# Second attention in turns of grouped heads, with transposed values, minima and masked scores on VectorE, and expert rows gathered in two groups

## What is computed

```python
    x = x + gb * _L0_ffn_ref(h, ...)
    ...
    h = _layernorm(x, axis=-1) * (1 + ca) + sa
    x = x + ga * _L1_attn_ref(h, ...)
    ...
    for qs in range(0, S, WINDOW):
        ...
        k_c = jnp.concatenate([k[:, :, :meta_end], k[:, :, ls:qe]], axis=2)
        ...
        scores = jnp.einsum('bhqd,bhkd->bhqk', q_c, k_c) * scale
        scores = jnp.where(allowed[None, None], scores, -jnp.inf)
        attn = jax.nn.softmax(scores, axis=-1)
        chunks.append(jnp.einsum('bhqk,bhkd->bhqd', attn, v_c))
```

## Time and profile before

| | us |
|---|---|
| median of three runs | 2404.34 (2399.58 to 2405.88) |
| the profiled execution, device time | 2407.0 |
| its span | 2405.2 |
| TensorE busy in the span | 2165.4 (90%) |
| VectorE, ScalarE, GpSimd busy | 1123.3, 766.4, 779.6 |

### The profile page before, as it was taken

How to read it: one execution, slowest core, us unless ns; L and a number is a source line. 1 busy time by engine, 2 the same in 40 slices (tenths; PEclk the granted TensorE clock), 3 DMA queues, 4 the chain that set the end, 5 groups by cost and what they waited for, 6 DMA issues and landing times. The chain is left out here.

```text
span 2405.2 us, 41150 instructions
## 1 busy us (share of the span) xinstructions
PE 2165.4 (90%) x11700; PEld 1492.4 (62%) x11702; DVE 1123.3 (47%) x2783; ACT 766.4 (32%) x1814; POOL 779.6 (32%) x1344
## 2 busy tenths in 40 slices
PE   4799877999999999999916999999994999999998
PEld 2676544555555555555504777777782887878787
DVE  2467575565552222222235676666543454343432
ACT  0233244222222222222202555444552332322322
POOL 0243302223333333333268766677312201101000
PEclk7899888999999999999957999999997999999999
DMA  7555542665565566656443222222001212222220
GB/s 243 183 203 199 218 125 84 195 201 176 183 203 183 191 214 203 203 189 221 136 150 89 72 56 57 72 71 72 2 1 53 70 62 79 62 73 67 72 68 27
DMA packets 122498, 302.21 MB, mean 126 GB/s; under 512 B 24864, under 2 KB 28576, under 8 KB 122272
## 3 DMA queue, kind: packets, MB, share of 16 engines
q1 hardware_dynamic: 73376, 179.04, 22.3%
q0 software_dynamic: 23040, 75.52, 11.1%
q10 hardware_dynamic: 25984, 46.38, 5.2%
HBM read 216.47 MB, written 83.36 MB: 125 GB/s over the span
## 5 line engine op out<-in xcount | busy, mean ns | idle before, releaser
L1167 PE MATMUL bank<-arena 128*128 x1272 | 446.4, 494 | 10.7 <-issue 9.2
L1167 PEld LDWEIGHTS bank<-arena 128*128 128x128 f32 x1272 | 229.8, 191 | 148.5 <-issue 17.9
L1184 PE MATMUL bank<-arena 96*128 x632 | 297.5, 593 | 0.0
L1288 DVE TENSOR_TENSOR arena<-bank,mod 128x512 f32<-128x512 f32 x158 | 109.3, 692 | 214.8 <-PE bank L1184 178.1
L1890 PE MATMUL bank<-x_hi,w_hi 128*128 128x512 f32 x512 | 200.8, 392 | 6.0 <-DVE x_lo L2023 6.0
L1890 PE MATMUL bank<-x_hi,w_lo 128*128 128x512 f32 x512 | 199.4, 389 | 0.0
L1890 PE MATMUL bank<-x_lo,w_hi 128*128 128x512 f32 x512 | 199.2, 389 | 0.0
L1283 DVE TENSOR_TENSOR arena<-arena,bank 128x192 f32<-128x192 f32 x159 | 56.3, 354 | 303.5 <-ACT arena L1205 303.1
L1200 ACT COPY arena<-bank 96x256 f32<-96x256 f32 x158 | 58.2, 368 | 423.2 <-issue 221.2
L1704 DVE TENSOR_REDUCE arena<-bank 128x1 f32<-128x272 f32 x256 | 112.1, 438 | 169.3 <-PE bank L1589 157.8
L1146 POOL DMA_INDIRECT arena<-h_moe,arena x160 | 158.5, 991 | 75.7 <-issue 73.0
(11 more groups left out here) (331 smaller groups left out, 4293.5 us busy)
## 6 DMA issues: line engine op xcount, KB each, us to landing
arena<-in_moe_up SPq DMA_DIRECT2D x64, 768.0 KB, 7.1
y_moe<-arena ACTq DMA_DIRECT2D x158, 256.0 KB, 2.7
y_moe<-mod SPq DMA_DIRECT2D x32, 1024.0 KB
ffn_arena<-in_ffn_up SPq DMA_DIRECT2D x64, 512.0 KB, 3.5
arena<-in_moe_down SPq DMA_DIRECT2D x64, 384.0 KB, 9.4
arena<-in_L_wmod SPq DMA_DIRECT2D x12, 1024.0 KB, 7.0
x_res<-in_L_attn_x SPq DMA_DIRECT2D x1, 4096.0 KB
h_moe<-arena SPq DMA_DIRECT2D x16, 256.0 KB, 6.7
```

The costliest lines, as they stand in the source:

```text
L1167: mm = nc.tensor.matmul(psum[2 + b][:, 0:2 * FI], xgT[:, b, k], up_ring[:, bass.ds((e % RING) * UPW + k * 2 * FI, 2 * FI)], start=(k == 0) ...
L1184: mm = nc.tensor.matmul(psum[6 + b][:], hiddenT[:, b, n], down_ring[:, bass.ds((e % RING) * DOWNW + n * C, C)], start=(n == 0), stop=(n == 1))
L1288: nc.vector.tensor_tensor(y[:, b], psum[6 + b][:], mod[:, 0, 5], ALU.mult).then_inc(y_out, 1)
```

## The change

The stage has seven steps in a turn (`g y p f s a w`) and all 22 turns are unrolled; the attention is split in `s` (scores, minima, exponentials) and `a` (turned probabilities, values) one turn later, and `w` comes one turn after that.

- Scores: four heads of a group lie in four blocks of 32 rows and go to four banks (`scores`). Keys are no longer copied into zeroed rows.
- Mask and maximum: VectorE adds the mask to the scores, negates, writes them to SBUF and takes the minimum in one instruction (`maxima`); ScalarE's exponential has scale -1. The meta columns are subtracted separately, and one exponential serves all heads.
- Probabilities are turned per group, four heads into a bank; ScalarE copies whole banks.
- Values: v stands, the turned probabilities of four heads move, the result comes out with channels in rows (`b_o`); a second set of matmuls with ones gives the sums in every row (`b_sum`). VectorE takes the reciprocal of the whole bank and multiplies into `oT`. Rows of `wo` are loaded in that order, and the transpose of the output is gone.
- Expert rows: all eight gathers of tile 0 stand first in the stage; for later tiles they are issued in two groups of four, each behind one wait and one spacer.
- Weights get their scale in turn `f == 0` instead of at the start. Buffers move to memory that is free in this stage.

```diff
+            VRING, GROUPS = 5, 6
...
-            wq, wkv, wo = cv(KC, C), cv(KC, 2 * NKV1 * HD), cv(KC, C)
+            wq, wkv, wo = cv(KC, C), cv(KC, 2 * NKV1 * HD), cv(HP, C)
...
-            kT = cv(NKV1, HP, KEYS1)
...
+            kT = cv(NKV1, KEYS1)
+            qT = cv(2, NKV1, P)
...
+            v = cv(VRING, NKV1, HD)
...
+            prob = cv(GROUPS, HP, KEYS1)
+            probT = cv(2, NKV1, HP, P)
+            metaT = cv(2, P)
...
+            def schedule(turn):
+
+                tile = lambda t: t if 0 <= t < NT else None
+                for m in range(-4, NT + 2):
+                    turn(g=tile(m + 4), y=tile(m + 3), p=tile(m + 2), f=tile(m + 1), s=tile(m), a=tile(m - 1), w=tile(m - 2))
...
+                def gather(t, js):
+
+                    if t:
+                        pool.wait_ge(y_sum, TOPK * (t - 1) + js[-1] + 1)
+                    absorb()
+                    for j in js:
+                        nc.gpsimd.indirect_dma_start(out=yg[:, j], out_offset=None, in_=y_moe,
+                                                     in_offset=bass.IndirectOffsetOnAxis(ap=pos_u[:, t, j:j + 1], axis=0)).then_inc(y_in[j], 16)
+
...
+                gather(0, range(0, TOPK))
+                st.did(nc.gpsimd.memset(kT[:], 0.0))
+                st.did(nc.gpsimd.memset(ones_f, 1.0))
+                st.settle()
+                pool.sem_inc(ready, 1)
...
+                        pool.wait_ge(xhat, w + 1)
...
+                    if g:
+                        gather(g, range(0, 4))
...
+                        pool.wait_ge(rope_in[p % 2], 16 * (p // 2 + 1))
+                        pool.wait_ge(q_rows, p + 1)
...
+                        rotate(p, slice(0, NHEAD), 0, NHEAD).then_inc(roped_q, 1)
+                    if g:
+                        gather(g, range(4, TOPK))
...
+                        pool.wait_ge(kv_rows, p + 1)
+                        rotate(p, slice(NHEAD, NQK), 2, NKV1).then_inc(roped, 1)
+                schedule(turn)
...
+                def exps(t, c):
+                    for r in range(HP):
+                        n = HP * c + r
+                        act.wait_ge(mx_done, NHEAD * t + n + 1)
+                        some = slot(t, c)[:, r, META:KEYS1]
+                        nc.scalar.activation(some, some, ACT.Exp, bias=nmx[:, t % 2, n:n + 1], scale=-1.0).then_inc(exp_done, 1)
+
+                def copy_pT(t, c):
+                    if t and c == 0:
+                        act.wait_ge(o_mm, 2 * NKV1 * t)
+                    for n, k in enumerate(chunks(t)):
+                        act.wait_ge(pT_mm, copies_before(t, c) + n + 1)
+                        copy(probT[:, k, c].rearrange("p r n -> p (r n)"), psum[4 + k][:]).then_inc(pT_out, 1)
+
...
+                def scores(t, c):
+                    if c == 0:
+                        pe.wait_ge(q_in, t + 1)
+                        pe.wait_ge(k_in, t + 1)
+                    pe.wait_ge(mx_done, NHEAD * t + HP * c)
+                    for r in range(HP):
+                        q = slice(HD * r, HD * r + HD)
+                        nc.tensor.matmul(psum[r][:, 0:KEYS1], qT[q, t % 2, c], kT[q, c], start=True, stop=True).then_inc(s_mm, 1)
+
+                def turn_probs(t, c):
+                    pe.wait_ge(exp_done, NHEAD * t + HP * c + HP)
+                    if c == 0 and t:
+                        pe.wait_ge(o_out, t)
+                    pe.wait_ge(pT_out, copies_before(t, c))
+                    for k in chunks(t):
+                        for r in range(HP):
+                            at = META + P * k
+                            mm = nc.tensor.transpose(psum[4 + k][:, r * P:(r + 1) * P], slot(t, c)[:, r, at:at + P], ident[:])
+                        mm.then_inc(pT_mm, 1)
+
+                def turn(g, y, p, f, s, a, w):
+                    if s is not None:
+                        scores(s, 0)
+                    if p is not None:
+                        pe.wait_ge(h_done, p + 1)
...
+                        for k in range(KC):
+                            mm = nc.tensor.transpose(bb[:, k * P:(k + 1) * P], h[:, k * P:(k + 1) * P], ident[:])
+                        mm.then_inc(hT_mm, 1)
+                    if f is not None:
+                        pe.wait_ge(roped_q, f + 1)
...
+                        for c in range(NKV1):
+                            mm = nc.tensor.transpose(ba[:, c * P:(c + 1) * P], qk[:, f % 2, HP * c:HP * c + HP].rearrange("p h d -> p (h d)"), ident[:])
+                        mm.then_inc(qT_mm, 1)
...
+                    if a is not None:
...
+                        turn_probs(a, 0)
+                    if p is not None:
...
+                        for k in range(KC):
+                            mm = nc.tensor.matmul(bb[:], hT[:, k], wq[:, k], start=(k == 0), stop=(k == KC - 1))
+                        mm.then_inc(q_mm, 1)
+                    if s is not None:
+                        scores(s, 1)
+                    if a is not None:
+                        turn_probs(a, 1)
+                    if p is not None:
+                        pe.wait_ge(q_rows, p + 1)
...
+                        mm.then_inc(kv_mm, 1)
+                    if s is not None:
+                        scores(s, 2)
+                    if a is not None:
+                        turn_probs(a, 2)
+                    if w is not None:
+                        pe.wait_ge(o_out, w + 1)
...
+                        for r in range(HP):
+                            mm = nc.tensor.matmul(ba[:], oT[:, r], wo[:, r], start=(r == 0), stop=(r == HP - 1))
+                        mm.then_inc(wo_mm, 1)
+                    if a is not None:
+                        turn_probs(a, 3)
+                    if s is not None:
+                        scores(s, 3)
+                    if a is not None:
+                        pe.wait_ge(meta_exp, a + 1)
...
+                        for n in range(2):
+                            mm = nc.tensor.transpose(bb[:, n * P:(n + 1) * P], prob_meta[:, a % 2, HM * n:HM * n + HM].rearrange("p h k -> p (h k)"), ident[:])
+                        mm.then_inc(pM_mm, 1)
+                    if f is not None:
+                        pe.wait_ge(kx_done, f + 1)
...
+                        if w is not None:
+                            pe.wait_ge(x_out, w + 1)
+                        for c in range(NKV1):
+                            mm = nc.tensor.transpose(ba[:, c * P:(c + 1) * P], kx[:, c].rearrange("p r d -> p (r d)"), ident[:])
+                        mm.then_inc(kT_mm, 1)
+                    if a is not None:
+                        pe.wait_ge(pT_out, copies_before(a + 1, 0))
+                        pe.wait_ge(pM_out, a + 1)
+                        for bank, local, meta in ((b_o, lambda k, c: v[:, keys_of(a, k) % VRING, c], lambda r, c: v_meta[:, c // 2, r, c % 2]),
+                                                  (b_sum, lambda k, c: ones_f, lambda r, c: meta_sum[:, r, c % 2])):
+                            for k in chunks(a):
+                                for c in range(NKV1):
+                                    nc.tensor.matmul(bank[HD * c:HD * c + HD], local(k, c), probT[:, k, c].rearrange("p r n -> p (r n)"),
+                                                     start=(k == 0), stop=False)
+                            for r in range(HP):
+                                for c in range(NKV1):
+                                    mm = nc.tensor.matmul(bank[HD * c:HD * c + HD, r * P:(r + 1) * P], meta(r, c), metaT[:, c // 2],
+                                                          start=False, stop=(r == HP - 1))
+                                    if r == HP - 1:
+                                        mm.then_inc(o_mm, 1)
...
+                def maxima(t, c):
+                    kind = t if t < 2 else 2 + t % 2
...
+                        before = HP * t + c - GROUPS
+                        dve.wait_ge(pT_mm, copies_before(before // HP, before % HP + 1))
+                    if t >= 2 and c == 0:
+                        dve.wait_ge(exp_done, NHEAD * (t - 1))
+                        dve.wait_ge(pM_mm, t - 1)
+                    for r in range(HP):
+                        n = HP * c + r
+                        dve.wait_ge(s_mm, NHEAD * t + n + 1)
+                        nc.vector.tensor_tensor_reduce(slot(t, c)[:, r], psum[r][:, 0:KEYS1], mask1[:, kind], -1.0, 3e38, ALU.add, ALU.min,
+                                                       accum_out=nmx[:, t % 2, n:n + 1]).then_inc(mx_done, 1)
+                    dve.wait_ge(mx_done, NHEAD * t + HP * c + HP)
+                    heads = slice(HP * c, HP * c + HP)
+                    nc.vector.tensor_tensor(prob_meta[:, t % 2, heads], nmx[:, t % 2, heads].unsqueeze(2).to_broadcast([P, HP, META]),
+                                            slot(t, c)[:, :, 0:META], ALU.subtract).then_inc(meta_sub, 1)
+
+                def add_expert(t, j):
```

(63 more changed lines are left out.)

492 lines of the change are left out of this document (134 added, 358 removed).

## The result

The changed kernel takes 2438.7 us (median, 2438.3 to 2442.8) against 2405.1 us before on the same chips: ratio 1.0146, 95% interval [1.0124, 1.0167]. It is slower by 34 us (1.5%, and the interval leaves no change out); the forecast was 7 us faster. The profiled execution spans 2435.1 us, before 2405.2.

The account below looks back on a forecast made before the run. No engine's sum but the order of a loop of waits was to bound the kernel, its steps summing to 32.9 us a turn against 33.15. Tile 4's x-hat -10, eleven turns -2, drain +5: net -7 us, 2397; range 2350 to 2450.

Parts of the forecast that it names:

- step (c): TensorE's query projection and the transposes ahead of it run at a low clock after little work: 2.6 us, from 0 to 3.7.
- rival 3: Value block's column tiles do not run side by side: 13 us, turn +7.9, 2520; fully in series 2650; chance 0.12.
- the term for a group of scores: TensorE scores of four heads side by side: 0.54 us a group, between 0.45 (perfect) and 1.8 (serial).
- (a): From the end of x-hat, GpSimd scales and shifts h and TensorE starts turning it: 3.2 us.
- (b): TensorE's h and q transposes, eight probability transposes and query projection: 5.4 us.
- (d): VectorE's query bias, second and third minima groups, expert additions, key and value bias, residual and hand-overs: 11.1 us.
- (e): TensorE's key transposes after the residual 0.44, value block 5.3, hand-over 0.2: 5.9 us.
- (f): VectorE's reciprocal 3.3, product 0.69, x-hat 0.54, gaps 0.2: 4.7 us.
- GpSimd's route: Second route through a turn, gathers, rotations, power, then x-hat: 31.4 us, hidden by 1.5 us; sets the four turns after tile 0.
- Rival 2: Loop slower through dear reciprocal, minima, clock and value block: 35.9 us, half likelier, 34.8; 2425; decides from about 33.9; chance 0.23.
- The fill: Stage start: eight gathers go first from about 1215.5, additions wait for nothing else; tile 0's x-hat at 1235, 14 us earlier.
- The drain: Stage end after tile 15's x-hat: 30.4, 20, 19.6, 17, 4.4 plus 1.6 for the clock: 93 us, +5.

Follow-up runs that it names:

- the run with the late second group: Changed kernel with each later tile's second gather group moved into the next turn, behind GpSimd's scale and shift of h: 2384.7 us, ratio 0.9901.
- the run with the memset: Changed kernel with a one-column VectorE memset ahead of the reciprocal, so that the memset waits for the value block: 2424.6 us, ratio 1.0086.

## Why the prediction was wrong

**What was right.** TensorE stops being the bound, with a busy share of 0.71 and one long gap a turn released by GpSimd at a low clock (0.53 in 1568 to 1578, forecast as step (c)). The loop goes through x-hat, query projection, value block and reciprocal. Column tiles run side by side: the value block took 5.39 us (forecast 5.3; the serial bound was 21.1, so four side by side gave 3.9 fold), which puts rival 3 out. The reciprocal took 3.36 us (forecast 3.3). The Trainium skill (VectorE: DVE Perf Modes, First, the fixed hardware budget; the prediction names the section ahead of it) gives it a repeat count of 8, by which the estimate was 4.3 us; the trace doesn't agree with eight cycles a column. Right by luck was the term for a group of scores: 0.54 us was worked out from 32 records, but a group has eight; it took 0.68 from start to start.

**The turn.** 34.1 us instead of 32.9, from the timeline above: (a) 2.7 (forecast 3.2); (b) and (c) together 6.8 (8.0: the clock cost only the transposes, the projection ran in 3.60 us); (d) 9.3 (11.1: minima follow each other every 0.36 us, not 0.52, since the reading of the accumulator lies beside the next one; the wait before the query bias was 3.0, forecast at about 6); (e) 7.1 (5.9: scores and transposes still stood between residual and value block); the hold 3.7 (no step had it); (f) 4.5 (4.7). The step that failed here is the hand-over in (e), "0.2 us": it took 3.7. Without the hold the loop takes 30.7 us (the run with the late second group), 2.2 below the forecast. That is shorter than GpSimd's route, and so the route that was to be "hidden by 1.5 us" is not hidden either: in the run with the memset the power ends last and the turn is 32.0.

**Rival 2** had the right side and its point of decision (33.9 us) was passed, but not by its mechanism: of its four dear ends none came. That its 2425 lies nearer to the 2438.7 than the forecast does is luck.

**GpSimd's route in the first turns.** Forecast 27.8, 28.2, 30.5, 31.4; measured 30.7, 33.6, 30.5, 30.9. That GpSimd's route sets them was right: x-hat of tile 1 and of tile 2 wait 12.6 us each for the power. Two sizes in it were not. From the spacer ahead of the first group to the end of x-hat it takes 18.6 us in both turns instead of 16.1, of which the first group of gathers is 6.4 instead of 4.5 and the second 5.1. And in the second turn the spacer comes 15.0 us after x-hat's end (the forecast leaves 12.1), since the scaling of the weights stands ahead of the additions on VectorE (L1658 to L1673, from 1271.7 to 1280.3), for which there was no term.

With the second group behind h these turns take 24.8, 27.2, 26.4 and 27.3, though GpSimd has the same work. So the sum wasn't the floor: the group stood ahead of the power, for which VectorE waited, and could wait itself. Moving it gives 20 us in these four turns and 31 in the regular part, of which the hold is 20.

**The fill.** Tile 0's x-hat came at 1240.5, not 1235, although its gathers began at 1212.96, 2.5 us before the stage's start in before. The additions, which were to "wait for nothing else", waited for their rows (the first starts at 1220.3, the last at 1234.0, each released by a landing), but the statistics were done at 1235.9. The rest is the same place in GpSimd's queue, here ahead of tile 0's power:

```profile
1239.93 0.59 POOL L1457 TENSOR_TENSOR arena<-arena,neg_half 128x1 f32<-128x1 f32 x1
1240.55 0.55 DVE L1725 TENSOR_SCALAR down_scale<-x_res,arena 128x512 f32<-128x512 f32 x1 [4.62 <-POOL arena L1457]
```

From the first gather to x-hat is 27.6 us here and 23.5 with the second group moved. The direction was right, the size was 8 instead of 14.

**The drain.** Forecast 93 from the end of x-hat, measured 104.3. The forecast's five terms (30.4, 20, 19.6, 17, 4.4 and 1.6 for the clock) count from product to product, since 4.4 is an output projection of 3.68 and a residual of 0.69, and the reciprocal is priced in the terms before it. Cut that way the trace has 30.2, 22.9, 22.0, 23.4 and 5.9. The term that failed most is the fourth, 17: the turn in which there are no scores left and every step follows the one before.

```profile
1814.00 1.94 PE L1554 MATMUL bank<-ident,arena 128*128 128x128 f32 x8 [4.30 <-issue]
1816.70 1.94 PE L1554 MATMUL bank<-ident,arena 128*128 128x128 f32 x8 [0.77 <-ACT arena L1497]
1821.14 4.57 PE L1608 MATMUL bank<-arena,mod 128*128 128x512 f32 x8
1825.75 0.69 DVE L1765 TENSOR_TENSOR x_res<-bank,x_res 128x512 f32<-128x512 f32 x1 [11.85 <-PE bank L1608]
1833.18 3.36 DVE L1717 RECIPROCAL mod<-bank 128x512 f32<-128x512 f32 x1 [6.74 <-PE bank L1641]
1837.32 5.09 PE L1608 MATMUL bank<-arena,mod 128*128 128x512 f32 x8 [4.25 <-DVE mod L1719]
```

TensorE stands still for 4.3 us beside the reciprocal, runs three groups of transposes in 1.94 us each instead of 1.09 (granted clock 0.64 from 1809.7 to 1824), waits 0.77 us for ScalarE's copies between them, and its output projections take 4.57 and 5.09 us instead of 3.60. The 1.6 us set for the clock and the overlap of the copies were the parts that were wrong. The reciprocal was in the sum, but it is a dear part of it: the run with a copy in its place gets 16.7 us back in the drain alone.

**Together.** Against the forecast's end of the stage, 1808: fill 5.5, first turns 7.7, regular turns 10.2, drain 11.3, sum 34.7 of the 35.1 us by which it ends later. The hold, 20 us, is larger than any of these, but the cheaper steps (c) and (d) had paid half of it. Of the fill's 5.5 the place of the power accounts for 4.6.
